# Squaring 46x46 matrices on four quarters of TensorE, with the linear term carried across partitions

## The reference

```python
def _moore_penrose_pinv(x, iters=PINV_ITERS):          # 6 iterations
    I = jnp.eye(x.shape[-1], dtype=x.dtype)
    denom = jnp.max(jnp.sum(jnp.abs(x), axis=-1)) * jnp.max(jnp.sum(jnp.abs(x), axis=-2))
    z = jnp.swapaxes(x, -1, -2) / denom
    for _ in range(iters):
        xz = x @ z
        z = 0.25 * z @ (13.0 * I - xz @ (15.0 * I - xz @ (7.0 * I - xz)))
    return z
...
out = attn1 @ (_moore_penrose_pinv(attn2) @ (attn3 @ v))
...
weights = jnp.einsum('bske,bsk->bse', mask, topk_weights)
h = jax.nn.relu(jnp.einsum('bsh,ehf->bsef', x, w1) + b1)
expert_out = jnp.einsum('bsef,efh->bseh', h, w2) + b2
return jnp.einsum('bseh,bse->bsh', expert_out, weights)
```

## Time and profile before

| | us |
|---|---|
| median of 3 runs | 722.22 (720.36 to 723.89) |
| the profiled execution's own time | 717.63 |
| its span, first to last instruction | 715.8 |
| PE busy | 689.8 (96%) |
| PEld busy | 593.4 (83%) |
| DVE busy | 381.4 (53%) |
| POOL busy | 302.0 (42%) |
| ACT busy | 239.9 (34%) |

### The profile page before, as it was taken

One profiled execution on the slowest core, in us unless ns is written; L12 is line 12 of the kernel. 1 busy time (PEld: TensorE's weight loads), 2 busy tenths in 40 slices (PEclk: granted clock), 3 DMA queues, 4 the chain that ended last, 5 costly groups with the idle time before them and its releaser, 6 DMA issues.

```text
span 715.8 us, 38807 instructions
## 1 busy us (share of the span) xinstructions
PE 689.8 (96%) x17423; PEld 593.4 (83%) x17423; DVE 381.4 (53%) x994; ACT 239.9 (34%) x453; POOL 302.0 (42%) x397
## 2 busy tenths in 40 slices
PE   1899999998999999999999999999999999999996
PEld 1688888876788788989898888899898989888875
DVE  4555555553453653655466466445655664564532
ACT  1355555543231231332223233323223241332342
POOL 3776666632742642642452353425426432432000
PEclk9999999999999999999999999999999999999999
DMA  2400000000000000000000000000000000000000
GB/s 58 131 13 11 10 10 10 2 3 3 4 5 5 4 4 5 4 4 4 14 4 4 14 4 5 3 15 5 4 4 14 4 4 14 5 4 4 12 12 10
DMA packets 8886, 7.99 MB, mean 11 GB/s; under 512 B 1676, under 2 KB 8228, under 8 KB 8740
## 3 DMA queue, kind: packets, MB, share of 16 engines
q1 hardware_dynamic: 6916, 3.09, 1.7%
q0 software_dynamic: 672, 2.12, 1.0%
q10 hardware_dynamic: 1152, 0.53, 0.3%
HBM read 4.26 MB, written 1.48 MB: 8 GB/s over the span
## 4 chain that ended last, share of the span: by engine, by line
PE 94%; issue 1%; DVE 1%; ACT 1%; POOL 1%; ACTq 0%; DMA 0%; DVEq 0%; POOLq 0%
PE bank L880 88%; PE bank L925 4%; PE bank L904 1%; PE bank L891 1%; PE bank L1030 0%; DMA bout_sb<-in_L_attn_b_out 0%; PE bank L1081 0%; PE bank L1042 0%; ACT hT L587 0%; DVE mx L673 0%; POOL rstd L335 0%; ACT L461 0%; DVE E L676 0%; ACT XT L496 0%; DVE nm L645 0%
## 5 line engine op out<-in xcount | busy, mean ns | idle before, releaser
L426 POOL TENSOR_TENSOR T<-Q,W 128x506 f32<-128x506 f32 x144 | 172.5, 1226 | 287.9 <-DVE W L743 265.6
L587 ACT ACTIVATE hT<-bank,b_sb 128x360 f32<-128x360 f32 x128 | 71.8, 561 | 254.1 <-PE bank L880 251.2
L752 DVE SCALAR_TENSOR_TENSOR P<-T,bank 128x506 f32<-128x506 f32 x144 | 95.7, 665 | 111.1 <-PE bank L880 106.9
L880 PEld LDWEIGHTS bank<-W 46*46 46x46 f32 x6144 | 136.8, 120 | 19.0 <-issue 18.2
L880 PEld LDWEIGHTS bank<-P 46*46 46x46 f32 x6144 | 137.2, 120 | 16.4 <-issue 9.8
L880 PE MATMUL bank<-P 46*46 46x46 f32 x6144 | 143.2, 205 | 1.9 <-ACT P L553 1.9
L880 PE MATMUL bank<-W 46*46 46x46 f32 x6144 | 142.8, 205 | 0.0
L743 DVE SCALAR_TENSOR_TENSOR W<-bank,P 128x506 f32<-128x506 f32 x144 | 95.4, 667 | 77.0 <-PE bank L880 76.9
L565 ACT ACTIVATE Q<-P 128x506 f32<-128x506 f32 x144 | 82.3, 606 | 69.1 <-DVE P L752 62.6
L880 PE MATMUL bank<-w_sb,hT 128*128 128x128 f32 x768 | 100.8, 282 | 0.0
L880 PEld LDWEIGHTS bank<-w_sb,hT 128*128 128x128 f32 x768 | 91.1, 192 | 4.8
(11 more groups left out here) (121 smaller groups left out, 616.8 us busy)
## 6 DMA issues: line engine op xcount, KB each, us to landing
w_sb<-in_L_ffn_w POOLq DMA_DIRECT2D x2, 1024.0 KB, 7.5
pat<-in_x SPq DMA_DIRECT2D x24, 60.0 KB
out<-outb SPq DMA_DIRECT2D x24, 60.0 KB
wqkv_sb<-in_L_attn_w_qkv ACTq DMA_DIRECT2D x1, 192.0 KB, 2.7
band<-scratch SPq DMA_DIRECT2D x2, 66.1 KB
cn<-in_consts ACTq DMA_DIRECT2D x1, 72.0 KB, 1.9
tokw_sb<-in_L_tok_W ACTq DMA_DIRECT2D x1, 64.0 KB, 2.8
tokb_sb<-in_L_tok_b ACTq DMA_DIRECT2D x1, 64.0 KB, 3.7
```

The lines of the kernel that those rows point to most:

```text
L426: pool.tensor_tensor(out=T[g], in0=Q[g], in1=W[g], op=ALU.subtract).then_inc(s_t[g], 1)
L587: act.activation(hT[e % 2][f][:, 0:BT], bank[4 + f][:, 0:BT], ACT.Relu, bias=b1_sb[:, 2 * e + f:2 * e + f + 1]).then_inc(s_hT, 1)
L752: dve.scalar_tensor_tensor(out=P[g], in0=T[g], scalar=T_OUT, in1=squared(g), op0=ALU.mult, op1=ALU.subtract).then_inc(s_p[g], 1)
L880: return pe.matmul(out, lhsT, rhs, start=start, stop=stop, skip_group_check=True)
```

## The change

The number of groups goes from 3 to 4, each of 8 slots and one bank. Groups are squared in pairs h (0 and 1, then 2 and 3), slot by slot in turn. Of each pair one group uses the quarters as before, and the other the two crossed ones: rows 0 to 63 into columns 64 to 127, and rows 64 to 127 into columns 0 to 63. So the four quarters of the array get one matmul each in turn. A crossed squaring leaves the result in the other half of the partitions. In even groups the square of P is crossed, in odd ones the square of W; the linear term has to follow, and so Q of the even groups and T of the odd groups are written half by half into the other half, with two instructions of 64 partitions for one of 128. W is now made from Q instead of P, with other constants, and signs change. T waits for the T before it, and GpSimd waits for its last T at the end of an iteration.

Four banks for the squares leave fewer for the rest: what used bank 3 uses bank 4, `up` banks 5 and 6, and `down` bank 7 alone, so that it waits for the `mix` of the expert before. `MIXES` moves the mixes of experts 0 to 5 one point earlier.

```diff
-CUT = (0, 11, 22, 32)
-NG = 3
+CUT = (0, 8, 16, 24, 32)
+NG = 4
...
-        MIXES = {3: 0, 4: 1, 6: 2, 7: 3, 9: 4, 10: 5, 11: 6, 12: 7}
+        MIXES = {2: 0, 3: 1, 5: 2, 6: 3, 8: 4, 9: 5, 11: 6, 12: 7}
...
                     pool.wait_ge(s_qs[g], n + 1)
                     pool.wait_ge(s_w[g], n + 1)
                     wait(pool, s_p[g], n)
-                    pool.tensor_tensor(out=T[g], in0=Q[g], in1=W[g], op=ALU.subtract).then_inc(s_t[g], 1)
+                    wait(pool, s_t[(g - 1) % NG], n + (g > 0))
+                    if g % 2 == 0:
+                        ins = pool.tensor_tensor(out=T[g], in0=Q[g], in1=W[g], op=ALU.add)
+                    else:
+                        for to, fro in swaps:
+                            ins = pool.tensor_tensor(out=T[g][to, :, :], in0=Q[g][fro, :, :], in1=W[g][fro, :, :],
+                                                     op=ALU.add)
+                    ins.then_inc(s_t[g], 1)
+                pool.wait_ge(s_t[NG - 1], n + 1)
...
                     wait(act, s_t[g], n)
-                    act.activation(Q[g], (P if k else P0)[g], ACT.Copy, scale=T_IN).then_inc(s_qs[g], 1)
+                    src = (P if k else P0)[g]
+                    if g % 2 == 0:
+                        for to, fro in swaps:
+                            ins = act.activation(Q[g][to, :, :], src[fro, :, :], ACT.Copy, scale=T_IN)
+                    else:
+                        ins = act.activation(Q[g], src, ACT.Copy, scale=T_IN)
+                    ins.then_inc(s_qs[g], 1)
...
                 for g in range(NG):
-                    dve.wait_ge(s_pp[g], n + 1)
-                    dve.scalar_tensor_tensor(out=W[g], in0=squared(g), scalar=S_SCALE, in1=(P if k else P0)[g],
+                    dve.wait_ge(s_qs[g], n + 1)
+                    dve.wait_ge(s_pp[g // 2], n + 1)
+                    dve.scalar_tensor_tensor(out=W[g], in0=Q[g], scalar=W_IN, in1=squared(g),
                                              op0=ALU.mult, op1=ALU.subtract).then_inc(s_w[g], 1)
...
-            def squares(g, t):
-
-                for s in range(CUT[g + 1] - CUT[g]):
-                    ins = pair(bank[g], s * NS, t[g][:, s, :], t[g][:, s, :])
+            def squares(h, t, crossed):
+
+                for s in range(SL):
+                    for g in (2 * h, 2 * h + 1):
+                        c = slice(s * NS, (s + 1) * NS)
+                        for a, (lo, hi) in enumerate(halves):
+                            to = halves[1 - a if g % 2 == crossed else a]
+                            ins = mm(bank[g][to[0]:to[1], c], t[g][lo:hi, s, :], t[g][lo:hi, s, :])
                 return ins
...
-                wait_apart(pe, met, (s_hT, 2 * j + 2), (s_mix, j - 1))
+                wait_apart(pe, met, (s_hT, 2 * j + 2), (s_mix, j))
...
-                        ins = mm(bank[6 + e % 2][:, t * D:(t + 1) * D], hT[e % 2][f][:, t * TT:t * TT + 128],
+                        ins = mm(bank[7][:, t * D:(t + 1) * D], hT[e % 2][f][:, t * TT:t * TT + 128],
```

More of the change, by code:

```diff
@@ L241, in tower @@
         s_p = [sem(f"s_p{g}") for g in range(NG)]
-        s_pp = [sem(f"s_pp{g}") for g in range(NG)]
+        s_pp = [sem(f"s_pp{h}") for h in range(NG // 2)]
         s_w = [sem(f"s_w{g}") for g in range(NG)]
@@ L245, in tower @@
         s_t = [sem(f"s_t{g}") for g in range(NG)]
-        s_ww = [sem(f"s_ww{g}") for g in range(NG)]
+        s_ww = [sem(f"s_ww{h}") for h in range(NG // 2)]
         s_r, s_o = sem("s_r"), sem("s_o")
@@ L591, in turned_weights @@
                 act.wait_ge(s_wtt, blk + 1)
-                act.activation(wT[:, 0:BT], bank[3][0:EXPERTS, 0:BT], ACT.Copy).then_inc(s_wT, 1)
+                act.activation(wT[:, 0:BT], bank[4][0:EXPERTS, 0:BT], ACT.Copy).then_inc(s_wT, 1)
             first_p()
@@ L843, in mix @@
                     wait(dve, s_out, 16 * TILES * blk)
-                y = bank[6 + e % 2][0:TT, 0:TILES * D].rearrange("p (t d) -> p t d", t=TILES)
+                y = bank[7][0:TT, 0:TILES * D].rearrange("p (t d) -> p t d", t=TILES)
                 for t in range(TILES):
@@ L1019, in p_squares, with w_squares @@
                         wait_apart(pe, met, (s_p[g], blk * ITERS + k))
-                    squares(g, P if k else P0).then_inc(s_pp[g], 1)
-            def w_squares(blk, k):
-                for g in range(NG):
+                squares(h, P if k else P0, 0).then_inc(s_pp[h], 1)
+            def w_squares(blk, k, h):
+                for g in (2 * h, 2 * h + 1):
                     wait_apart(pe, met, (s_w[g], blk * ITERS + k + 1))
-                    squares(g, W).then_inc(s_ww[g], 1)
+                squares(h, W, 1).then_inc(s_ww[h], 1)
             def turn_out(blk):
@@ L1029, in turn_out @@
                 for u in range(UN):
-                    ins = pe.transpose(bank[3][:, u * 128:(u + 1) * 128], O[:, u, :], ident)
+                    ins = pe.transpose(bank[4][:, u * 128:(u + 1) * 128], O[:, u, :], ident)
                 ins.then_inc(s_ot, 1)
@@ L1035, in project @@
                 for t in range(TILES):
-                    ins = mm(bank[3][:, t * D:(t + 1) * D], OT[:, t * TT:t * TT + 128], wout_sb[:, :])
+                    ins = mm(bank[4][:, t * D:(t + 1) * D], OT[:, t * TT:t * TT + 128], wout_sb[:, :])
                 ins.then_inc(s_pr, 1)
@@ L1108, in _ @@
                             results(blk)
-                        elif j % 2 == 0:
-                            p_squares(blk, j // 2)
-                        else:
-                            w_squares(blk, j // 2)
+                        else:
+                            for h in range(2):
+                                (w_squares if j % 2 else p_squares)(blk, j // 2, h)
                     if d is not None and j in DOWNS:
```

43 lines of the change are left out of this document (22 added, 21 removed).

## The result

The changed kernel took 713.19 us (median of 4, 710.21 to 715.79) beside 721.29 us for the kernel before: ratio 0.988, 95% interval 0.983 to 0.993. It is faster, by 1.2%, where 9.8% were forecast (651 us, 618 to 702).

The account below looks back on a forecast made before the run. TensorE was taken to bound the kernel, and after the change the loop T, P, W about equally. Savings of 5 x 11.0 + 12.4 + 3.5 + 4.4 = 75.3 us, less 4.4 at the ends, gave 651 us, range 618 to 702.

Parts of the forecast that it names:

- The squarings: On TensorE, four quarters work at once, so a squaring of 128 MATMULs takes 1.45 us instead of 2.90.
- Rival A: On TensorE, four quarters go no faster than two; gain zero, about 727 us; chance 0.14.
- B: On TensorE, half the effect: 2.1 to 2.3 us per squaring as weight loads conflict, time near 685; chance 0.08.
- Feeding: TensorE's instruction supply: 13.6 ns per MATMUL and weight load allows 1.75 us per squaring at worst; 1.45 taken.
- The loop: T on GpSimd, then P and W on VectorE, with handovers: 7.2 us per iteration, T 6.05 of it.
- the self-wait: On GpSimd, each T waits for the T before it: 0.1 us taken, bounds 0 and 0.2.
- the walk: Followed each iteration's first T through a block with experts, adding delays to the loop: 53.8 us instead of 64.8.
- Rival C: Clock falls to 1.2 GHz in blocks 0 and 1, where TensorE idles: +34 us, 685; chance 0.04.
- blocks 0 and 1: Blocks without experts, set by the loop: about 49 us instead of 52.6, and 51.1 instead of 55.5.
- The ends: Start +0.4 us for two P0; tail +4 (bounds 2 and 7), as successive `down` on one bank wait about 1.1.

Follow-up runs that it names:

- e4: Changed kernel with one matrix squared repeatedly behind the tail on one, two and four quarters; four settle at 27 ns per MATMUL and weight load.
- e5: Changed kernel plus the filler, a useless 512-column matmul between the halves of each squaring of P; 713.33 us, ratio 0.990 to the kernel before.
- e6: e3 plus the filler of e5 between the halves of each squaring of P; 683.98 us, ratio 0.948 to the kernel before.
- e3: Changed kernel with all squarings on the two diagonal quarters and every second slot left unsquared; 703.86 us, ratio 0.973 to the kernel before.
- e14: e3 with T and Q of all groups written whole, four instructions instead of six; 622.90 us, ratio 0.866 to the kernel before.

## Why the prediction was wrong

The direction was right, and that four quarters work at once; what was wrong is how fast they can be fed, and the time was 62 us over the forecast.

- **The squarings.** Nearly right: read to the next work, as the 2.90 was, an unbroken squaring takes 1.65 us where 1.45 was taken, 0.2 x 96 = 19 us of TensorE's time. Rival A fell, and B with it: e4 shows no pairing that costs more. The Trainium skill ("TensorE: Matmul & The Clock Gate", Wait — 56ns, not 53.3ns?) has a floor of about 25 ns from start to start. In bursts the trace contradicts it with 12 ns; the sustained 27 ns of e4 are near it, but are a mean over pieces of 128 MATMULs, 12 to 22 ns apart, and the stalls between them, so that it is another limit.
- **Feeding: the step that failed.** "So feeding alone allows 1.75 us at the worst, and probably less, because the queue was filling up. I take 1.45." The 88 instructions of the earlier trace rows came after an idle stretch, out of what had been fetched already: in that trace no fetch stands between 158.91 and 169.67 us. They show what a burst can do, not what can be kept up: 256 instructions per 3.47 us, 27 ns a pair instead of 13.6. Before the change a pair took 22.7 ns in a squaring but far more in the matmuls between, and the mean over a block, 64.8 us for 3704 instructions or 4.5 us for 256, left slack. After it 53.8 us were forecast, 3.7 us for 256, against 3.47 at the best and 4.0 between neighbouring stalls of the changed kernel, with bursts at twice the pace of supply. This cost 17 to 29 of the 62 us (e5 to e6).
- **The loop.** Mis-sized: 7.2 forecast, 8.4 at k = 3 and 5. T takes 6.4 instead of 6.05, the self-wait near its upper bound (0.17 of 0.2), and so a quiet loop 7.6. And the walk left out the mix at k = 2 and k = 4. VectorE's timeline in e3, free of stalls, at full clock:

```profile
396.15 0.54 DVE L769 SCALAR_TENSOR_TENSOR P<-T,bank 128x368 f32<-128x368 f32 x1 [1.61 <-POOL T L432]
396.61 0.86 DVE L863 SCALAR_TENSOR_TENSOR acc<-bank,wt,acc 120x128 f32<-120x128 f32 x3
397.39 1.87 DVE L760 SCALAR_TENSOR_TENSOR W<-Q,bank 128x368 f32<-128x368 f32 x4
```

  Between the last P and the first W stand 397.39 - 396.61 = 0.8 us of mix. In e6 the first T come at 1.8, 10.0, 20.7, 29.1, 38.2 and 46.6 and the block ends at 56.8; forecast were 1.9, 9.3, 19.8, 27.0, 36.2 and 53.8: 3.0 us a block, 15 in five blocks. Of these, 0.6 a block is the filler's, since in e3 the T of k = 1 comes at 9.4. That the loop held the blocks where there was no filler is shown by e14, where 2 us less per iteration took them from 57.1 and more (e3) to 49.5. In e6 the filler fills TensorE as well, so that its 3.0 us can't be put on the loop alone.
- **Rival C** was given 0.04 and a place in blocks 0 and 1. The clock fell in every block, most of all in these. Where supply isn't the limit, lifting it with the filler gains 20 us (e3 to e6); in the change itself it brings nothing, net of the filler's work (e5). Blocks 0 and 1 take 58.3 and 56.0 in e6 (forecast 49 and 51.1), so that 14 us more of the miss stand there; 17 and 14 us of them were at 1.2 GHz, but how much of the 14 is the clock's and how much the loop's wasn't told apart.
- **The ends.** 0.6 us at the start (0.4 forecast). The tail, from the end of the last block (654.74) on, takes 57.2 us instead of 51.0: 6.2 more, where 4 was taken with bounds of 2 and 7; 4.2 us for two `down` instead of 2.84, 1.4 for the 1.1 taken.

Together, by medians: e5 to e6, mostly supply, is 29 us, and e6 lies 33 above the forecast; that makes the 62, as e5 and the changed kernel take the same time. This counts the clock's cost and the filler's as cancelling, which only their sum shows. The profiled run of e6 is 36 us above the 646.7 forecast for a profiled run: 17 in blocks 2 to 6 (15 as above and 2 where the clock was low), 14 in blocks 0 and 1, 3 in block 7 (55.5 us for 52.4) and 2 in the tail.

A version with T in halves but without GpSimd's self-waits wasn't tried: the instructions would touch the same tiles unordered.

## What to carry to other kernels

Before a change packs more small matmuls into the same time, count TensorE's instructions per stage and hold them against the sustained supply (here 256 per 3.47 us at the best, nearer 4 in the changed kernel), not against the pace of a burst. Where two limits lie close together, size both before crediting one: here each edit alone gave 9 to 22 us and the two together 90. And walk every in-order engine instruction by instruction between the operation that a loop ends on and the one it starts with, since what stands between them was free only as long as the loop was covered.

## What the runs showed of the hardware that I had not expected

TensorE's instructions come in fetches of 16 KB, 256 instructions, and those of a fetch that TensorE stands waiting for start 1.3 to 1.5 us after its record ends. In e4 one fetch follows another at 3.47 us at the best (1.2 GHz), and the one piece at full clock was no faster, 3.74.

In e4 the clock stayed at 1.2 GHz through 35 us, from 706.4 to 741.6, in which TensorE had hardly a gap: three runs of 10.4 us on pairs of quarters, each followed by two MATMULs of 512 columns (2.07 us). Windows over the first and the third pairing:

```profile
706.40:716.80 10.40, 10.40 (x257) 10.32 (x256) 0.00 (x0) 0.00 (x0) 0.00 (x0) 0.50 0.02 3
731.30:741.70 10.40, 10.40 (x258) 10.31 (x257) 0.00 (x0) 0.00 (x0) 0.00 (x0) 0.50 0.01 3
```

Busy 10.40 of 10.40 us, granted 0.50; it rose at 744.3, 0.7 us after all four quarters had gone to work, and fell again at 751.1 after the supply stalls had begun. So here a TensorE without gaps did not get the clock back. In the kernel before, where pairs of quarters stood between full matmuls, it was 1.00 for the whole block.
